# A two-layer graph attention kernel: the next step's exponentials taken directly behind ScalarE's copy of the sums

## The chip, the cores and the metric

One Trainium2 chip, one core of it. The metric is the device time of one execution in microseconds (us). The engines are named as the profile names them: PE is TensorE (PEld its weight loads), DVE is VectorE, ACT is ScalarE, POOL is GpSimd, SP is SyncE.

## What is computed

A graph with 6250 nodes and 106250 edges (50000 drawn edges in both directions and one loop per node), the edges sorted by their destination. A first stage applies a layer norm and a ReLU, a second one runs an equivariant convolution over all edges, and then two graph attention layers follow. The change touches only these last two, each of which computes, with 4 heads of 64 features:

```python
z = (x @ W).reshape(n, HEADS, ODIM)
el = jnp.sum(z * al, axis=-1)
er = jnp.sum(z * ar, axis=-1)
e = jax.nn.leaky_relu(el[src] + er[dst], negative_slope=NEG_SLOPE)
e_max = jax.ops.segment_max(e, dst, num_segments=n)
ex = jnp.exp(e - e_max[dst])
denom = jax.ops.segment_sum(ex, dst, num_segments=n)
alpha = ex / denom[dst]
msg = z[src] * alpha[:, :, None]
out = jax.ops.segment_sum(msg, dst, num_segments=n)
out = jax.nn.elu(out + x.reshape(n, HEADS, ODIM) + b.reshape(HEADS, ODIM))
```

## The kernel before, in words

The four stages (`front_stage`, `conv_stage`, `gat_stage` for layer 0 and for layer 1) run one after the other, each with a block of instructions of its own for every engine. In `gat_stage` the edges are taken in groups of 8 tiles of 128 edges, one group a step; a step adds its group's sums to a window of 128 nodes. A layer has 104 steps. Four steps make a quad, and a quad also finishes one block of 256 nodes, whose work is spread over its four steps r = 0 to 3. The loop (`all_steps`, L816 to L822) has one quad as its body, 25 times round, and the last quad is written out behind it, with `ahead` telling how many steps still follow. The order on each engine is written out by hand, and engines meet through semaphores alone.

Step v on each engine, as far as the change and the prediction speak of it:

- **POOL** (L1649 to L1657) gathers the rows of z for the step four ahead, in two groups of 4 indirect DMAs: the even tiles once PE has done its first half of the sums of the step whose buffer is reused (`half_summed`), the odd tiles once PE has done the second half (`part_summed`).
- **ACT** (L1605 to L1631) waits for `diff_ready` and takes two exponentials: L1609 of the 128 x 36 differences of score and maximum, which are the edges' weights `ex`, and L1610 of 36 x 1 values, the factor `fac` by which older sums are rescaled. Then it copies the transposed one-hots of step v + 2 (L1577), stages the indices of step v + 4 (L831), makes 8 weighted one-hots (L1619, for half of the odd tiles), waits until PE has summed the whole step, and copies PE's sums out of PSUM (L1624). Behind the copy stand the node block's work, which are three passes over 128 x 512 at r = 1 (L1581, L1583, L1585, the ELU's exponential) and in layer 0 one copy of table rows at r = 2 and at r = 3 (L1591), and the staging of step v + 4 (L839, L840, L842).
- **DVE** (L2011 to L2054) waits for the first exponential, makes the other weighted one-hots (L1927: two instructions for the first half of the sums, one for the second), folds the step before into its window (L1934 to L1943), and prepares the steps ahead: one-hots (L1855, L854), scores (L1880, L1883), the segment maxima by scans, the differences of step v + 1 (L1919, which raises `diff_ready`), and the first scans of step v + 2 (L1890, L1891). At r = 0 it takes the denominators' reciprocals early in the step and the node block's state at its end.
- **PE** (L1802 to L1828) makes the sums of the 8 tiles in two halves, `tile_sums` (16 matmuls at L1732 and 4 at L1737 each). The first half needs DVE's two weighted one-hots, and stands behind the window sums of the step before (L1746, L1748) and a small one for the scans (L1697); the second half needs DVE's third and ACT's eight. Between the halves stand L1705, L1684 and L1677. Behind the second half, L1711 hands DVE the transposed maxima of step v + 1.

So a step's differences are ready only shortly after PE has finished the sums of the step before, which is what ACT's copy waits for too.

Of the kernel before, what the change touches and what calls it, by code (L numbers as in the profile page):

```python
# [20 lines left out]
ACT = mybir.ActivationFunctionType  # L21
# [1349 lines left out]
def gat_stage(nc, m, layer):  # L1371
# [8 lines left out]
    with ExitStack() as ctx:  # L1380
# [3 lines left out]
        def sb(name, shape, dt=F32):  # L1384
            return ctx.enter_context(nc.sbuf_tensor(f"ge{layer}_" + name, shape, dt))
# [12 lines left out]
        def scratch(width, parts=P):  # L1398
            a = m.scratch[0:parts, free_scratch[0]:free_scratch[0] + width]
            free_scratch[0] += width  # L1400
            assert free_scratch[0] <= SCRATCH
            return a
# [22 lines left out]
        diff = [scratch(LANES) for u in range(2)]  # L1425
        ex = [scratch(LANES) for u in range(2)]
# [5 lines left out]
        fd = [sb(f"fd{u}", [LANES, 1]) for u in range(2)]  # L1432
        fac = [sb(f"fac{u}", [LANES, 1]) for u in range(2)]
# [137 lines left out]
        @block.scalar  # L1571
        def _(act):
            last_quad = load_last_quad(act, m)

            def copy_hotT(v):
                act.wait_ge(hotT_ps, v + 1)
                nc.scalar.copy(hotT, ps_hotT[:, 0:2 * P]).then_inc(hotT_ready, 1)  # L1577

            def exponential(k, b=node):
                act.wait_ge(s_v, k + 1)  # L1580
                nc.scalar.activation(b.h, b.x, ACT.Relu, scale=-1.0).then_inc(s_neg, 1)  # L1581
                act.wait_ge(s_neg, k + 1)
                nc.scalar.activation(b.h, b.h, ACT.Exp, scale=-1.0).then_inc(s_ex, 1)  # L1583
                act.wait_ge(s_ex, k + 1)
                nc.scalar.activation(b.ps[:, :], b.h, ACT.Copy, bias=-1.0).then_inc(s_em, 1)  # L1585

            def rows(k, t):
                act.wait_ge(s_pZ, k * 2 + (t + 1))
                if t == 0:
                    act.wait_ge(st_rows, k * 16 + 16)  # L1590
                nc.scalar.copy(node.rows[:, t * ZW:(t + 1) * ZW], ps_node[:, 0:ZW]).then_inc(s_rows, 1)  # L1591

            def last_rows(k, t, b):
                act.wait_ge(s_pZ, k * 2 + (t + 1))
                if t == 0 and b is node:
                    act.wait_ge(st_rows, k * 16 + 16)
                nc.scalar.copy(b.rows[:, t * ZW:(t + 1) * ZW], b.tables[t][:, 0:ZW]).then_inc(s_rows, 1)

            groups = [stage_sources(nc, act, m, r, idx[r], idx_ready) for r in range(4)]
            for r in range(4):  # L1600
                stage_places(nc, act, m, r, groups[r], staged[r], columns[r], staged_ready)
            for v in range(2):
                copy_hotT(v)

            def step(quad, r, ahead):  # L1605
                v = quad * 4 + r
                u = r % 2
                act.wait_ge(diff_ready, v + 1)
                nc.scalar.activation(ex[u], diff[u], ACT.Exp).then_inc(ex_ready, 1)  # L1609
                nc.scalar.activation(fac[u][:, :], fd[u][:, :], ACT.Exp).then_inc(ex_ready, 1)  # L1610
                if ahead >= 2:
                    copy_hotT(v + 2)
                if ahead >= 4:
                    group = stage_sources(nc, act, m, v + 4, idx[r], idx_ready)
                act.wait_ge(part_summed, v + 4)
                act.wait_ge(ex_ready, v * 2 + 2)
                for k in range(G // 2 + 1, G, 2):
                    for h in range(HEADS):
                        ins = nc.scalar.activation(weighted(k, h), one_hot(r, k), ACT.Copy,  # L1619
                                                   scale=ex[u][:, h * (G + 1) + k:h * (G + 1) + k + 1])  # L1620
                ins.then_inc(hots_act_ready, 1)
                act.wait_ge(part_summed, v + 5)
                act.wait_ge(summed, v + 1)
                nc.scalar.copy(sums, ps_part[:, 0:D + HEADS]).then_inc(sums_ready, 1)  # L1624
                if r == 1:
                    exponential(quad)
                if r >= 2 and layer == 0:
                    rows(quad, r - 2)
                if ahead >= 4:
                    act.wait_ge(pick_ready, v + 1)  # L1630
                    stage_places(nc, act, m, v + 4, group, staged[r], columns[r], staged_ready)  # L1631

            all_steps(act, last_quad, step)
            first, lead = load_rest(act, m, last_quad)
            with act.Fori(first, REAL, 2) as n:
                k = n + lead
                exponential(k)
                exponential(k + 1, second)
                if layer == 0:
                    for t in range(2):  # L1640
                        last_rows(k, t, node)
                    for t in range(2):
                        last_rows(k + 1, t, second)
# [488 lines left out]
```

## Time and profile before

| | us |
|---|---|
| three runs | 4824.91, 4825.26, 4829.48 |
| their median | 4825.26 |
| span of the profiled execution, first to last instruction | 4824.0 |
| first start of a layer 0 gather (L1655) | 1904.1 |
| ACT busy in the span | 1279.2 |
| POOL busy in the span | 2537.5 |

No time of its own is listed for the profiled execution beside its span; the span lies 1.26 us under the median of the runs. In the profile an operation is named by its line, engine and kind, then what it writes and reads (the small buffers all lie in `scratch`, the gathered rows in `nodes`). A row of the timeline gives its start, its duration, and in brackets how long the engine had been idle before it and what ended that; several like instructions in a row are merged (x8), and matmuls of 32-bit data count twice. "remote" in the brackets means that the profile found no engine's instruction that ended the wait at that time, "issue" that it found no wait at all. Ends of matmuls are modelled.

### The profile page before, as it was taken

What the parts mean: (1) busy time and instruction counts of PE and PEld (TensorE: products, weight loads), DVE (VectorE), ACT (ScalarE), POOL (GpSimd) and SP (SyncE); (2) the same over time, 40 slices, a digit from 0 to 9 for tenths busy, and PEclk for the clock granted to TensorE, in tenths of its full rate; (3) what the DMA queues carried; (4) which work ended last, traced back from release to release, by engine and by line L of the source; (5) the groups of instructions that cost most, each with busy time, mean ns of one, the idle gap of its engine ahead of it and who ended that gap; (6) DMA issues with size and microseconds to landing.
All of it is one profiled execution on the core that took longest, in us unless ns stands there. A gap on an engine that the chain in (4) does not pass through costs nothing. (4 is left out here: it accounts for less than half of the span.)

```text
span 4824.0 us, 104766 instructions
## 1 busy us (share of the span) xinstructions
PE 3342.4 (69%) x33932; PEld 2406.6 (50%) x33933; DVE 2350.8 (49%) x7219; ACT 1279.2 (27%) x4694; POOL 2537.5 (53%) x2630
## 2 busy tenths in 40 slices
PE   6567766676667775677777776666576776767676
PEld 4334444444444444455555555555455555555555
DVE  6445444444544444445444444444344554444455
ACT  5112211212212212233333333323222222222232
POOL 6444444444444443555555555553655555555553
PEclk9777777777777777555555555555555555555555
DMA  7222222222222222333333333332333333333332
GB/s 231 78 79 83 78 75 80 80 79 81 81 78 81 77 80 84 88 99 94 94 98 93 98 96 94 96 94 75 96 93 102 94 94 94 97 99 93 94 93 82
DMA packets 241750, 442.92 MB, mean 92 GB/s; under 512 B 83665, under 2 KB 134933, under 8 KB 241567
## 3 DMA queue, kind: packets, MB, share of 16 engines
q0 software_dynamic: 119808, 334.13, 25.4%
q1 hardware_dynamic: 121887, 108.14, 7.3%
q8 instruction: 25, 0.41, 0.0%
q14 instruction: 30, 0.25, 0.0%
HBM read 381.95 MB, written 60.10 MB: 92 GB/s over the span
## 5 line engine op out<-in xcount | busy, mean ns | idle before, releaser
L1655 POOL DMA_INDIRECT nodes<-z_rows,scratch x1664 | 1644.4, 988 | 1272.8 <-issue 415.7
L1101 POOL DMA_INDIRECT scratch<-h_rows,scratch x832 | 818.8, 984 | 941.7 <-DVE nodes L1251 716.0
L1732 PE MATMUL ge_part<-nodes,scratch 128*32 128x64 f32 x13312 | 472.6, 313 | 243.2 <-DVE scratch L1927 133.5
L1624 ACT COPY scratch<-ge_part 128x260 f32<-128x260 f32 x208 | 78.3, 376 | 1851.5 <-remote 1665.8
L1145 PE MATMUL ce_part<-nodes,scratch 128*32 128x128 f32 (+1 forms) x6656 | 456.7, 394 | 126.2 <-issue 113.4
L1732 PEld LDWEIGHTS ge_part<-nodes,scratch 128*32 128x32 f32 x13312 | 359.4, 167 | 296.5 <-issue 153.2
L1145 PEld LDWEIGHTS ce_part<-nodes,scratch 128*32 128x32 f32 x6656 | 256.5, 140 | 331.5 <-issue 279.2
L1279 DVE TENSOR_TENSOR nodes<-nodes,ce_sum 128x512 f32 x105 | 72.3, 689 | 707.6 <-remote 367.0
L1737 PE MATMUL ge_part<-scratch 128*32 128x4 f32 x3328 | 209.9, 200 | 261.5 <-issue 259.3
L1746 PE MATMUL ge_sum<-scratch 128*128 128x128 f32 x832 | 243.6, 445 | 208.4 <-ACT scratch L1624 208.2
L1919 DVE TENSOR_TENSOR scratch<-scratch,ge_runs 128x32 f32<-128x32 f32 x208 | 44.0, 212 | 692.4 <-remote 675.5
L1125 PE MATMUL ce_w<-fc_sb,scratch 64*128 64x256 f32 x1664 | 304.2, 495 | 109.3 <-ACT scratch L1020 96.3
L1155 PE MATMUL ce_sum<-nodes 128*128 128x128 f32 x832 | 167.5, 364 | 305.7 <-issue 217.6
L1251 DVE TENSOR_TENSOR nodes<-ce_w,scratch 128x768 f32<-128x768 f32 x416 | 377.2, 949 | 0.0
L1619 ACT ACTIVATE scratch<-scratch 128x32 f32<-128x32 f32 x1664 | 376.3, 312 | 0.1
L1927 DVE TENSOR_TENSOR scratch<-scratch 128x256 f32<-128x256 f32 x624 | 244.3, 419 | 233.8 <-ACT ge_fac L1610 137.3
L1125 PEld LDWEIGHTS ce_w<-fc_sb,scratch 64*128 64x128 f32 x1664 | 183.3, 236 | 277.0 <-issue 175.2
L1737 PEld LDWEIGHTS ge_part<-scratch 128*32 128x32 f32 x3328 | 187.8, 166 | 263.9 <-issue 261.5
L1155 PEld LDWEIGHTS ce_sum<-nodes 128*128 128x128 f32 x832 | 141.8, 257 | 349.1 <-issue 247.6
L1746 PEld LDWEIGHTS ge_sum<-scratch 128*128 128x128 f32 x832 | 184.4, 309 | 228.8 <-ACT scratch L1624 227.0
L1059 ACT COPY nodes<-ce_part 128x512 f32<-128x512 f32 x104 | 61.0, 586 | 804.5 <-remote 738.0
L1717 PEld LDWEIGHTS ge_sum<-ge_fac,lane_sel 36*128 36x128 f32 x832 | 184.0, 306 | 80.9 <-issue 76.5
(269 smaller groups left out, 5802.1 us busy)
## 6 DMA issues: line engine op xcount, KB each, us to landing
nodes<-z_rows,scratch POOLq DMA_INDIRECT x1664
nodes<-hT SPq DMA_DIRECT2D x56, 256.0 KB
scratch<-h_rows,scratch POOLq DMA_INDIRECT x832
z_rows<-scratch SPq DMA_DIRECT2D x28, 264.0 KB
z_rows<-nodes SPq DMA_DIRECT2D x28, 264.0 KB
hT<-scratch SPq DMA_DIRECT2D x28, 256.0 KB
hT<-nodes SPq DMA_DIRECT2D x28, 256.0 KB
nodes<-x_rows SPq DMA_DIRECT2D x28, 256.0 KB
```

Of the source, the lines that this page charges most:

```text
L1101: nc.gpsimd.indirect_dma_start(xg[u][:, i * D:(i + 1) * D], None, m.h_rows, bass.IndirectOffsetOnAxis(ap=idx[r][:, k:k + 1], axis=0)).then ...
L1125: ins = nc.tensor.matmul(ps_w[q][:, 2 * half + a, :, :].rearrange("p k f -> p (k f)"), hidT[u][rows, col:col + P], m.fc1[rows, :], start=T ...
L1145: ins = nc.tensor.matmul(here, hots[u][:, at:at + TW], these, start=(q == 0 and c == 0), stop=(q == 1), skip_group_check=True)
L1155: ins = nc.tensor.matmul(ps_sum[:, c, :], sums[:, c * P:(c + 1) * P], pick[u], start=(c == 0), stop=True, skip_group_check=True)
L1251: ins = V.tensor_tensor(out[:, :, 1 + 3 * k:4 + 3 * k, :], w[:, :, 2 + k:3 + k, :].broadcast_to([P, UNIT, 3, MUL]), x[:, :, 1:4, :], ALU.mult)
L1619: ins = nc.scalar.activation(weighted(k, h), one_hot(r, k), ACT.Copy, scale=ex[u][:, h * (G + 1) + k:h * (G + 1) + k + 1])
L1655: nc.gpsimd.indirect_dma_start(zg[r][:, k * ZW:(k + 1) * ZW], None, m.z_rows[layer], bass.IndirectOffsetOnAxis(ap=idx[r][:, k:k + 1], axis ...
L1717: nc.tensor.matmul(ps_sum[u][:, FAC + c:FAC + c + 1], m.lane_sel[:, c * P:(c + 1) * P], fac[u][:, :], start=(c == 0), stop=True, skip_grou ...
L1732: ins = nc.tensor.matmul(ps_part[j * TW:(j + 1) * TW, h * HF:(h + 1) * HF], weighted(k, h), zg[r][:, k * ZW + h * HF:k * ZW + (h + 1) * HF ...
L1737: ins = nc.tensor.matmul(ps_part[j * TW:(j + 1) * TW, D:D + HEADS], one_hot(r, k), lanes(ex[r % 2])[:, k, :], start=False, stop=(q == 1), ...
L1746: nc.tensor.matmul(ps_sum[u][:, c * NW:(c + 1) * NW], sums[:, c * P:(c + 1) * P], pick[u], start=False, stop=True, skip_group_check=True)
L1927: return V.tensor_tensor(out, one.broadcast_to([P, NB // 2, HEADS, TW]), by.broadcast_to([P, NB // 2, HEADS, TW]), ALU.mult)
```

## The change

The two exponentials become a helper. They are taken once for step 0 ahead of the loop, and then in step v for step v + 1, directly behind the copy of the sums and ahead of the node block's work and the staging, in place of standing first in the next step.

```diff
--- before.py
+++ after.py
@@ -1602,12 +1602,16 @@
             for v in range(2):
                 copy_hotT(v)
 
+            def exponentials(v, u):
+                act.wait_ge(diff_ready, v + 1)
+                nc.scalar.activation(ex[u], diff[u], ACT.Exp).then_inc(ex_ready, 1)
+                nc.scalar.activation(fac[u][:, :], fd[u][:, :], ACT.Exp).then_inc(ex_ready, 1)
+
+            exponentials(0, 0)
+
             def step(quad, r, ahead):
                 v = quad * 4 + r
                 u = r % 2
-                act.wait_ge(diff_ready, v + 1)
-                nc.scalar.activation(ex[u], diff[u], ACT.Exp).then_inc(ex_ready, 1)
-                nc.scalar.activation(fac[u][:, :], fd[u][:, :], ACT.Exp).then_inc(ex_ready, 1)
                 if ahead >= 2:
                     copy_hotT(v + 2)
                 if ahead >= 4:
@@ -1622,6 +1626,8 @@
                 act.wait_ge(part_summed, v + 5)
                 act.wait_ge(summed, v + 1)
                 nc.scalar.copy(sums, ps_part[:, 0:D + HEADS]).then_inc(sums_ready, 1)
+                if ahead >= 1:
+                    exponentials(v + 1, 1 - u)
                 if r == 1:
                     exponential(quad)
                 if r >= 2 and layer == 0:
```

Semaphores and buffers are the same, and the order on PE, DVE, POOL and SP is what it was. Names of lines shift: L1609 and L1610 become L1607 and L1608, L1619 becomes L1623, L1624 becomes L1628, and lines behind them grow by 6.

ACT, layer 0, from the last instruction ahead of the loop into its first step; before:

```order
L818 UNCONDITIONAL_BRANCH
L818 ISA
L1609 ACT_TABLE_LOAD
L1609 ACTIVATE scratch<-scratch 128x36
L1610 ACTIVATE ge_fac<-ge_fd 36x1
L1576 REGISTER_ALU
L1577 COPY scratch<-ge_hotT 128x256
L131 ISA
L131 TENSOR_LOAD tab
```

and now:

```order
L1577 COPY scratch<-ge_hotT 128x256 x2
L1607 ACT_TABLE_LOAD
L1607 ACTIVATE scratch<-scratch 128x36
L1608 ACTIVATE ge_fac<-ge_fd 36x1
L818 UNCONDITIONAL_BRANCH
L818 ISA
L1577 COPY scratch<-ge_hotT 128x256
L131 ISA
L131 TENSOR_LOAD tab
```

Exponentials and the load of ACT's function table in front of them (ACT_TABLE_LOAD) stood inside the loop, behind the branch at L818, and now stand ahead of it; no table load is left inside the loop. In layer 1 there was none and there is none.

ACT, layer 0, end of step r = 1 and start of the next: the staging and the exponentials before (the three node passes L1581 to L1585 stand between the copy L1624 and these rows),

```order
L839 ACTIVATE scratch<-dst_sb,minus_base 128x8
L840 ISA
L840 ACTIVATE scratch<-first,minus_base 128x5
L842 ISA
L842 COPY scratch<-pick_cols 128x128
L1609 ACTIVATE scratch<-scratch 128x36
L1610 ACTIVATE ge_fac<-ge_fd 36x1
L1577 COPY scratch<-ge_hotT 128x256
```

and now, from the copy of the sums on:

```order
L1628 COPY scratch<-ge_part 128x260
L1607 ACTIVATE scratch<-scratch 128x36
L1608 ACTIVATE ge_fac<-ge_fd 36x1
L1580 REGISTER_ALU
L1581 ACTIVATE nodes<-nodes 128x512
L1583 ACTIVATE nodes<-nodes 128x512
L1585 ACTIVATE ge_node<-nodes 128x512
```

The two exponentials have moved up past the node passes and the staging; the copy of the one-hots (L1577) follows the staging directly.

## Rows read from the trace of the kernel before

**Rows 1.** The page, part 1: busy time and share of each engine.
```profile
PE 3342.4 (69%) x33932; PEld 2406.6 (50%) x33933; DVE 2350.8 (49%) x7219; ACT 1279.2 (27%) x4694; POOL 2537.5 (53%) x2630
```

**Rows 2.** Waits of engines, one for another, 2505 to 3160 us (layer 0).
```profile
ACT scratch L1624 <- remote: 418.8, 45, 12.0
DVE scratch L1919 <- remote: 172.8, 45, 4.1
```

**Rows 3.** Timeline of ACT, layer 0: start us, us, operation.
```profile
2518.89 0.38 ACT L1624 COPY scratch<-ge_part 128x260 f32<-128x260 f32 x1 [9.70 <-remote]
...
2521.80 0.23 ACT L1609 ACTIVATE scratch<-scratch 128x36 f32<-128x36 f32 x1
...
2522.38 1.81 ACT L1619 ACTIVATE scratch<-scratch 128x32 f32<-128x32 f32 x8
2532.47 0.38 ACT L1624 COPY scratch<-ge_part 128x260 f32<-128x260 f32 x1 [8.28 <-remote]
...
2545.96 0.38 ACT L1624 COPY scratch<-ge_part 128x260 f32<-128x260 f32 x1 [9.62 <-remote]
```

**Rows 4.** Timeline of DVE over the same stretch.
```profile
2518.93 0.21 DVE L1919 TENSOR_TENSOR scratch<-scratch,ge_runs 128x32 f32<-128x32 f32 x1 [3.81 <-remote]
...
2519.44 0.39 DVE L1891 TENSOR_TENSOR_SCAN scratch<-scratch,ge_eT 36x128 f32<-36x128 f32 x1
2522.15 0.82 DVE L1927 TENSOR_TENSOR scratch<-scratch 128x256 f32<-128x256 f32 x2 [2.33 <-ACT ge_fac L1610]
```

**Rows 5.** Timeline of PE over the same stretch.
```profile
2521.00 0.39 PE L1697 MATMUL ge_runs<-perm,scratch 36*1 36x36 f32 x4
2523.03 1.08 PE L1732 MATMUL ge_part<-nodes,scratch 128*32 128x64 f32 x32 [1.64 <-DVE scratch L1927]
...
2527.11 1.08 PE L1732 MATMUL ge_part<-nodes,scratch 128*32 128x64 f32 x32
...
2535.12 1.08 PE L1732 MATMUL ge_part<-nodes,scratch 128*32 128x64 f32 x32 [0.17 <-issue]
```

**Rows 6.** Timeline of POOL over the same stretch.
```profile
2519.67 0.95 POOL L1655 DMA_INDIRECT nodes<-z_rows,scratch  x1 [1.87 <-remote]
...
2523.44 1.06 POOL L1655 DMA_INDIRECT nodes<-z_rows,scratch  x1 [0.30 <-issue]
2526.55 0.95 POOL L1655 DMA_INDIRECT nodes<-z_rows,scratch  x1 [2.05 <-PE ge_part L1737]
...
2530.33 0.95 POOL L1655 DMA_INDIRECT nodes<-z_rows,scratch  x1 [0.31 <-issue]
```

**Rows 7.** Timeline at the end of layer 0, past the last gather.
```profile
3314.24 1.04 POOL L1655 DMA_INDIRECT nodes<-z_rows,scratch  x1 [0.30 <-issue]
...
3328.31 1.08 PE L1732 MATMUL ge_part<-nodes,scratch 128*32 128x64 f32 x32
...
3329.52 0.38 ACT L1624 COPY scratch<-ge_part 128x260 f32<-128x260 f32 x1 [5.43 <-PE ge_part L1737]
```

**Rows 8.** L1609 over the whole run: duration ns min/median/max, first and last start.
```profile
L1609 ACT ACT_TABLE_LOAD  x25: 1283/1283/1283, 1917.8 to 3256.7; - x25
```

**Rows 9.** Timeline of ACT: copies 48 steps apart, in layers 0 and 1.
```profile
2505.37 0.38 ACT L1624 COPY scratch<-ge_part 128x260 f32<-128x260 f32 x1 [8.58 <-remote]
...
3159.59 0.38 ACT L1624 COPY scratch<-ge_part 128x260 f32<-128x260 f32 x1 [8.51 <-remote]
...
3968.96 0.38 ACT L1624 COPY scratch<-ge_part 128x260 f32<-128x260 f32 x1 [9.44 <-remote]
...
4621.76 0.38 ACT L1624 COPY scratch<-ge_part 128x260 f32<-128x260 f32 x1 [9.45 <-remote]
```

**Rows 10.** Timeline of DVE at a turn of the loop, layer 0 and layer 1.
```profile
2549.13 0.76 DVE L1927 TENSOR_TENSOR scratch<-scratch 128x256 f32<-128x256 f32 x2 [2.21 <-issue]
...
3794.58 0.76 DVE L1927 TENSOR_TENSOR scratch<-scratch 128x256 f32<-128x256 f32 x2 [1.26 <-ACT ge_fac L1610]
```

**Rows 11.** L1655 over the whole run, durations ns min/median/max.
```profile
L1655 POOL DMA_INDIRECT nodes<-z_rows,scratch x1664: 951/957/1622, 1904.1 to 4776.1; - x185
```

## The prediction

> **What bounds the kernel now.** I read the page first. No engine is full: over the span PE shows 69% and POOL 53%, and ACT, the engine that is reordered, 27% [rows 1]. ACT is thus short of work, and the question is only whether its two exponentials stand on the path that sets the length of a step. The view of waits says what ACT spends its time on: in 655 us of layer 0 it sat 418.8 us in front of its copy of the sums, in 45 waits of up to 12 us each, ended by something that the profile calls remote; DVE sat 172.8 us in front of the differences, again 45 times [rows 2]. Both wait for PE to finish a step's sums, at the same moment: the copy starts at 2518.89, the differences at 2518.93 [rows 3, 4].
>
> Next I laid the timelines of one step side by side. I call an interval the time from one copy of the sums to the next. The interval from 2518.89 to 2532.47 follows r = 1, so that ACT's node passes and staging stand between the copy and the exponential at 2521.80 [rows 3]. DVE's weighted one-hots follow at 2522.15, after 2.33 us of idling that ACT ended [rows 4], and PE's first half of the sums at 2523.03, after 1.64 us of idling that DVE ended [rows 5]. That is a visible chain from the exponential to PE, and it is what the change shortens.
>
> But what comes behind it does not follow PE's start. The second half starts at 2527.11 [rows 5] and the copy that waits for it only at 2532.47 [rows 3], 5.36 us later. Where no gather is running any more, behind the last of layer 0 at 3314.24, the same second half goes from 3328.31 to its copy at 3329.52, in 1.21 us [rows 7]. So some 4 us of every second half are not PE's own work. What stands beside them is POOL: its group of four gathers begins at 2526.55, the last of them begins at 2530.33 and ends at 2531.28 [rows 6], and 1.19 us after that end the copy is released. The group before runs from 2519.67 to 2524.50, and the group behind it starts 2.05 us later, released by PE [rows 6]. POOL thus alternates: four gathers at a pace of 1.26 us, PE's release about a microsecond behind their end, 2 us of gap, the next four. Two groups are (2530.33 - 2526.55) + (2523.44 - 2519.67) + 0.95 + 1.06 = 9.56 us, two gaps of about 2 us make the rest of 13.6. I read this as a step that is set by the gathers: PE's sums end when a group of gathers has drained, however long ago they were started. The trace doesn't say by what means the gathers hold PE back, and the forecast doesn't need it.
>
> **A test that lies in the trace.** The next interval, from 2532.47 to 2545.96, follows r = 2. ACT has less in front of its exponential there, and PE starts the first half at 2535.12 [rows 5], 2.65 us behind the copy, against 4.14 us in the interval before. PE is 1.49 us earlier and the interval is 13.49 us long against 13.58 [rows 3]: 0.09 us for 1.49.
>
> **The change, part by part.**
>
> 1. *Exponentials at r = 1, both layers (26 intervals each, 52).* The copy ends at 2519.27, the differences at 2519.14 [rows 3, 4], so the exponential will start around 2519.4 and not at 2521.80, some 2.4 us earlier. DVE is occupied with its scans until 2519.83 [rows 4], so its one-hots start near 2519.9. PE ends what stands in front of its sums at 2521.39 [rows 5]; that is late next, and the first half can start 2523.03 - 2521.39 = 1.64 us earlier. On the path this would be 52 x 1.64 = 85 us. By the test above it is nothing, or at the most 1.64 x 0.09/1.49 = 0.10 us an interval, 5 us in all. I take 0: the group of gathers ends at 2524.50, behind the time at which PE's first half, started at 2523.03 and 1.08 us long, stops showing work.
> 2. *Exponentials at r = 2 and r = 0.* At r = 2 PE starts the sums at 2535.12 with 0.17 us of idling [rows 5]; there is nothing to win but that. At r = 0 DVE has the node block's state in front of the one-hots, which the change leaves alone. 0.
> 3. *The turn of the loop (r = 3), layer 0.* The change takes 25 loads of ACT's function table, 1.283 us each, out of the loop [rows 8] and leaves one ahead of it. ACT is relieved by 24 x 1.283 = 31 us. At the turn DVE idles 2.21 us in front of the one-hots in layer 0 and 1.26 us in layer 1, where there is no table load [rows 10]; so DVE will be about 0.95 us earlier in layer 0. What the earlier start is worth is shown by the two layers: 48 steps of layer 0 take 3159.59 - 2505.37 = 654.22 us, the same number of layer 1 takes 4621.76 - 3968.96 = 652.80 us [rows 9]. The difference, 1.42 us in 12 quads, is 0.118 us a quad and 3.0 us in 25 quads. It holds everything in which the layers differ, the copies of table rows too, so 3.0 is at the upper end of what fits the pace of the gathers; a lower end is 0, and 31 us if each load were on the path. I take 3.0, since its row is of the very same step without the load.
> 4. *What is pushed back.* At r = 1 the node passes and the staging now start behind two short exponentials and a possible wait for the differences. The total of ACT's work up to the eight one-hots is the same, these therefore stay near 2522.4 to 2524.2, and the second half that needs them starts at 2527.11 [rows 3, 5]: 2.9 us of cover. Were that cover gone, each us of delay would count in full. The indices that POOL needs are staged ahead of these eight, four steps before their gathers. Where the differences come later than the copy, ACT waits for them with the staging and node work queued behind; ACT idles 8.28 us ahead of the next copy [rows 3], which hides this. 0. In the first step, and in the last four of each layer, gathers don't hide everything; there PE's own queue is next, and I take 0 with 1 us either way.
> 5. *Order on POOL, SP, PE.* No instruction of theirs moves, no DMA is issued earlier or later by order. 0.
>
> The sum: 4824.0 - 3.0 = 4821.0 us for the profiled span. The median of the runs stands 1.26 us over that span, so **4822 us**.
>
> Here the page and the Trainium skill differ on one price. The trace has the table load at 1.283 us [rows 8], and the exponential behind it is delayed by that and no more, as far as DVE's 0.95 us tell. The Trainium skill, "ScalarE: Activation LUTs", section "What ACT_TABLE_LOAD costs", gives the same 1283 ns and adds a drain of about 1380 ns, 2.66 us for each switch of set; by it ACT would be relieved by some 64 us and not 31, and the sum would still be the same, since the term goes by the two layers' pace. The measured row decides.
>
> **The rivals.**
>
> *The exponentials are on the path (faster).* For it speaks the chain of rows 4 and 5, in which the idling of DVE and PE ends with ACT's exponential. Against it speak the 5.36 us against 1.21 us and the interval at r = 2. Price: 85 us from part 1, and 0.95 x 25 = 24 us at the turn of layer 0: 4825 - 109 = 4716 us.
>
> *The table loads count in full (faster).* If at the turn of the loop ACT and not the gathers set the time, 24 x 1.283 = 31 us go: 4825 - 31 = 4794 us. Against it: then a turn in layer 0 would cost over a microsecond more than in layer 1, and not 0.118.
>
> *DVE falls on POOL's gathers (slower).* Gathers take 0.951 us at the least, 0.957 in the middle, and 1.622 us in the worst case [rows 11]; one in the rows above took 1.06 [rows 6]. With DVE's one-hots up to 2.2 us earlier at r = 1, and 0.95 at the turn, DVE works beside other gathers than now. If in each of these 52 + 25 = 77 intervals one gather more grew by half the way to that worst case, 0.33 us, and POOL's groups set the pace, the kernel would take 77 x 0.33 = 25 us more: 4825 + 25 = 4850 us. It decides from the point where the growth falls into the second group, which nothing compensates. Against it: the same instructions already run beside gathers in all intervals, and there is as much chance of an overlap going away. The Trainium skill, "GPSIMD Engine Reference", section "1. Specifications", says that GpSimd shares its SBUF interfaces with VectorE and contends with instructions that have two SBUF inputs, which L1927 has; it is this rival's mechanism, and the spread of rows 11 agrees with it without proving it.
>
> **How the numbers follow.** A measurement of this kernel can tell about 0.2% from no change, 9.65 us: faster is under 4815.6, slower over 4834.9. The gathers' pace, as forecast: 0.81. Exponentials on the path, 4716: 0.06. Table loads in full, 4794: 0.05. DVE on the gathers, 4850: 0.08. The forecast's own range is from 4822 - 5 (part 1's upper end) - 2 - 3 of doubt in the turn, 4812, to 4822 + 3 (part 3 worth nothing) + 2, and the runs' own 4 us of spread, 4831. To take in a part of the slower rival, with some gathers grown, the range goes to 4836; below, to 4809. That leaves out the two faster rivals and most of the slower one, under 0.2. Chances: faster 0.13 (both faster rivals and the lowest edge of the forecast), slower 0.08, same 0.79.
>
> **What would show it.** In the changed profile at r = 1 the exponential should stand about 0.5 us behind the copy, DVE's one-hots about 1.0 us and PE's first half about 2.5 us, against 4.14 now. No table load should remain in the quads of layer 0. If I am right, the intervals are still 13.5 to 13.6 us long, PE's second half starts about 8.3 us behind the copy, and ACT's wait in front of its copy is longer by what it saved. I am wrong if the second half starts earlier with the first and the intervals shrink by more than 0.1 us, or if gathers of the second group show well over 1 us where they showed 0.96.

## The result, and the profile after

The changed kernel takes 4861.84 us (median of 4 runs, 4858.3 to 4878.06), the kernel before 4825.09 us beside it (4 runs, 4821.57 to 4829.48). The ratio is 1.0071, 95% interval 1.0048 to 1.0095: **slower by about 34 us**, where 4822 us and no change were forecast. The profiled execution took 4859.04 us with a span of 4857.2 us, 33.2 us over the span before.

Two names first. POOL's four gathers right behind a copy of the sums fetch the odd tiles; I call them the *odd group* (the expectations below say "second group"). The four after them are the *even group*. Both can be seen in [rows 6]: the odd one from 2519.67, the even one from 2526.55.

The page after, part 1, answers to [rows 1]:

```profile
PE 3343.5 (69%) x33932; PEld 2410.4 (50%) x33933; DVE 2341.0 (48%) x7219; ACT 1269.3 (26%) x4670; POOL 2595.6 (53%) x2630
```

All instruction counts but ACT's (24 table loads fewer) are those of before, ACT and DVE are busy for 10 us less, and POOL for 58.1 us *more*. The gathers themselves (timings of L1661, which was L1655; [rows 11] before) and the table loads ([rows 8] before), each line by its own view:

```profile
L1661 POOL DMA_INDIRECT nodes<-z_rows,scratch x1664: 951/957/1750, 1906.9 to 4805.0; - x185
```

```profile
L1607 ACT ACT_TABLE_LOAD  x1: 1283/1283/1283, 1920.8 to 1920.8; - x1
```

The shortest and the middle gather are what they were; so some few got longer. The timeline of POOL behind the copy at 2526.21, a copy of r = 1, shows which (start, duration, operation, idle before and what ended it):

```profile
2526.99 1.64 POOL L1661 DMA_INDIRECT nodes<-z_rows,scratch  x1 [1.63 <-remote]
2528.94 0.96 POOL L1661 DMA_INDIRECT nodes<-z_rows,scratch  x1 [0.31 <-issue]
...
2531.46 0.96 POOL L1661 DMA_INDIRECT nodes<-z_rows,scratch  x1 [0.30 <-issue]
2534.25 0.95 POOL L1661 DMA_INDIRECT nodes<-z_rows,scratch  x1 [1.83 <-remote]
...
2540.87 1.75 POOL L1661 DMA_INDIRECT nodes<-z_rows,scratch  x1 [1.89 <-remote]
```

It is the first gather of the odd group: 1.64 us where [rows 6] has 0.95, and 1.75 us behind the next copy. The timeline of DVE tells what stands beside it:

```profile
2526.24 0.21 DVE L1925 TENSOR_TENSOR scratch<-scratch,ge_runs 128x32 f32<-128x32 f32 x1 [3.59 <-remote]
2527.07 0.73 DVE L1933 TENSOR_TENSOR scratch<-scratch 128x256 f32<-128x256 f32 x2
2528.74 0.22 DVE L1903 TENSOR_TENSOR_SCAN scratch<-scratch,ge_runs 1x36 f32<-1x36 f32 x1 [0.94 <-PE ge_runs L1703]
```

DVE's two weighted one-hots begin 0.86 us behind the copy and 0.08 us behind the gather. Before, they began at 3.26 us [rows 3, 4], when that gather was long done. PE's timeline, and ACT's copies of the sums from here on:

```profile
2528.64 1.08 PE L1738 MATMUL ge_part<-nodes,scratch 128*32 128x64 f32 x32
...
2533.94 1.08 PE L1738 MATMUL ge_part<-nodes,scratch 128*32 128x64 f32 x32
```

```profile
2512.28 0.38 ACT L1628 COPY scratch<-ge_part 128x260 f32<-128x260 f32 x1 [11.51 <-PE ge_part L1743]
2526.21 0.38 ACT L1628 COPY scratch<-ge_part 128x260 f32<-128x260 f32 x1 [9.71 <-remote]
2526.49 0.23 ACT L1607 ACTIVATE scratch<-scratch 128x36 f32<-128x36 f32 x1
...
2540.09 0.38 ACT L1628 COPY scratch<-ge_part 128x260 f32<-128x260 f32 x1 [8.48 <-remote]
...
2548.19 0.38 ACT L1628 COPY scratch<-ge_part 128x260 f32<-128x260 f32 x1 [4.06 <-PE ge_part L1743]
...
2567.26 0.38 ACT L1628 COPY scratch<-ge_part 128x260 f32<-128x260 f32 x1 [11.56 <-PE ge_part L1743]
```

The exponential stands 0.28 us behind the copy and PE's first half 2.43 us, so at r = 1 everything that was to become earlier did. The intervals are now 13.93, 13.88, 8.10 and 19.07 us: a quad of 54.98 us. Before, the medians of the four intervals of layer 0 are 13.56, 13.55, 13.49 and 13.75, together 54.35. The short and the long one (27.17 us) are no longer than their two before (27.24); it is the other two that grew, by 0.3 to 0.4 us each. Such a pair of a short and a long interval is not new: in layer 0 of the trace of before, every third quad has one, behind r = 1 and r = 2 (the copies at 2409.67, 2419.09 and 2437.15 are 9.42 and 18.06 us apart). New is how often: of the 84 intervals counted below, 22 of layer 0 are shorter than 12.9 us, and 7 were before. DVE's and PE's lead is gone by the even group: that starts at 2534.25, 8.04 us behind the copy, against 7.66 in [rows 3, 6].

Where the 33.2 us lie, by the copies of each layer: 10.2 and 9.1 us in the 84 steps between the 13th and the 97th copy (layers 0 and 1), 3.3 us in the first 12 steps of the two, 8.9 us in the last 7, 2.3 us ahead of the first copy, where nothing was changed, and -0.6 us in what is left. The stretch ahead of the first copy comes and goes between executions: in the four profiles taken on the first chip below, which differ only behind it, it takes 1967.0 to 1986.1 us. So the 84 steps are the finer measure below (12 steps, or three quads, are a full period of the rhythm, and 84 are seven): from the 13th copy's start to the 97th copy's, 1145.0 and 1142.1 us before, 1155.2 and 1151.1 us after.

### The profile page after: what moved, and what is told of

It reads as the page before. It is cut to its first block and busy times, and to the rows that moved or that the text cites. A ratio compares the mean times of both kernels' runs of the same rounds, so it can differ in the third digit from the quotient of the medians.

```text
span 4857.2 us, 104690 instructions
## 1 busy us (share of the span) xinstructions
PE 3343.5 (69%) x33932; PEld 2410.4 (50%) x33933; DVE 2341.0 (48%) x7219; ACT 1269.3 (26%) x4670; POOL 2595.6 (53%) x2630
## 5 line engine op out<-in xcount | busy, mean ns | idle before, releaser
L1661 POOL DMA_INDIRECT nodes<-z_rows,scratch x1664 | 1702.4, 1023 | 1240.8 <-issue 409.3
L1738 PE MATMUL ge_part<-nodes,scratch 128*32 128x64 f32 x13312 | 526.4, 313 | 220.5 <-issue 181.5
L1628 ACT COPY scratch<-ge_part 128x260 f32<-128x260 f32 x208 | 78.2, 376 | 1818.3 <-remote 1253.6
L1145 PE MATMUL ce_part<-nodes,scratch 128*32 128x128 f32 (+1 forms) x6656 | 443.7, 385 | 138.4 <-issue 123.9
L1738 PEld LDWEIGHTS ge_part<-nodes,scratch 128*32 128x32 f32 x13312 | 385.1, 165 | 299.0 <-issue 258.3
L1623 ACT ACTIVATE scratch<-scratch 128x32 f32<-128x32 f32 x1664 | 375.3, 308 | 8.6 <-issue 8.5
L1690 PE MATMUL ge_er<-scratch 128*128 128x16 f32 x832 | 219.7, 359 | 83.0 <-issue 81.7
L1690 PEld LDWEIGHTS ge_er<-scratch 128*128 128x128 f32 x832 | 202.7, 315 | 93.0 <-issue 89.0
L1743 PE MATMUL ge_part<-scratch 128*32 128x4 f32 x3328 | 165.5, 203 | 104.4 <-issue 103.4
```

The lines of the kernel that those rows point to most:

```text
L1145: ins = nc.tensor.matmul(here, hots[u][:, at:at + TW], these, start=(q == 0 and c == 0), stop=(q == 1), skip_group_check=True)
L1661: nc.gpsimd.indirect_dma_start(zg[r][:, k * ZW:(k + 1) * ZW], None, m.z_rows[layer], bass.IndirectOffsetOnAxis(ap=idx[r][:, k:k + 1], axis ...
L1690: ins = nc.tensor.matmul(ps_er[:, q * W:(q + 1) * W], hotT[:, q * P:(q + 1) * P], er4, start=(q == 0), stop=True, skip_group_check=True)
L1738: ins = nc.tensor.matmul(ps_part[j * TW:(j + 1) * TW, h * HF:(h + 1) * HF], weighted(k, h), zg[r][:, k * ZW + h * HF:k * ZW + (h + 1) * HF ...
L1743: ins = nc.tensor.matmul(ps_part[j * TW:(j + 1) * TW, D:D + HEADS], one_hot(r, k), lanes(ex[r % 2])[:, k, :], start=False, stop=(q == 1), ...
```

## The experiments

**Theory 1**: DVE's two weighted one-hots (each a product of two operands in SBUF), moved over the first odd gather, stretch it, and the gathers set the pace. **Theory 2**: PE's earlier first half is what costs. **Theory 3**: the loss is made at the turn of the loop, or by the table load's new place. The runs come from three chips: the first four of the table from one on which the kernel before takes 4839.9 us, the next four from a second (4737.2 us), and the last eight, in two sets, from a third (4734.8 and 4732.0 us). Each ratio is against runs of the kernel before in the same set. Profiles are compared within a set, or between the last two chips, whose speed is the same; the first chip has no profile of the kernel before, and only_r3 stands in for it.

| run | first odd gather, us | 84 steps, layers 0 and 1, us | ratio, 95% interval |
|---|---|---|---|
| only_r3 | 0.95 | 1142.9, 1140.8 | 1.0011 (0.9998 to 1.0025) |
| only_r1 | 1.64 | 1150.5, 1147.9 | 1.0029 (1.0012 to 1.0047) |
| only_r2 | 1.74 | 1148.7, 1144.1 | 1.0044 (1.0031 to 1.0058) |
| hold | 1.64 | 1155.5, 1149.5 | 1.0074 (1.0052 to 1.0097) |
| x_two | 1.30 | 1128.7, 1126.1 | 0.9991 (0.9981 to 1.0001) |
| x_psum | 0.95 | 1127.9, 1125.6 | 0.9994 (0.9981 to 1.0008) |
| psum_before | 0.95 | 1128.0, 1127.0 | 0.9997 (0.9985 to 1.0008) |
| psum_after | 0.95 | 1128.4, 1127.6 | 1.0006 (0.9993 to 1.0019) |
| before_again | 0.95 | 1127.5, 1124.7 | - |
| after_again | 1.64 | 1138.1, 1133.5 | 1.0069 (1.0049 to 1.0088) |
| psum_after_again | 0.95 | 1128.4, 1128.2 | 1.0004 (0.9992 to 1.0017) |
| x_same | 1.30 | 1128.3, 1127.3 | 1.0006 (0.9996 to 1.0016) |
| x_next | 1.30 | 1128.1, 1127.0 | 1.0001 (0.9989 to 1.0012) |
| x_long | 2.31 | 1145.2, 1142.1 | 1.0084 (1.0065 to 1.0102) |
| only_r1_again | 1.64 | 1133.6, 1134.2 | 1.0050 (1.0034 to 1.0067) |
| psum_r3 | 0.95 | 1127.9, 1127.1 | 1.0014 (1.0003 to 1.0024) |

(The gather is the median behind the copy that the experiment is about: r = 2 in only_r2, the turn in only_r3, r = 1 in the others. In only_r2 it is 1.74 us in two quads of three and 0.95 us in the third. Kernels without the loss differ by up to 3.5 us in the 84 steps of a layer from one profile to the next in the same set, so less than that says nothing.)

**Which part of the change costs.** The helper's early call is kept for one r alone, the others stand where they stood before (here r = 1; only_r2 and only_r3 likewise):

```diff
             def step(quad, r, ahead):
...
+                if r in (1, 3, 0, ):
+                    exponentials(v, u)
...
-                if ahead >= 1:
+                if ahead >= 1 and r in (1, ):
                     exponentials(v + 1, 1 - u)
```

> Exponentials early only at the turn of the loop (behind r = 3), which also takes ACT's table load out of the loop. Theory 1 (DVE's one-hots run over the first gather of POOL's second group and stretch it): at the turn DVE is held by its own branch until about 2.2 us behind the copy, so nothing collides; first gather of the group 0.95 to 1.0 us, time 4819 to 4825 us. Theory 2 (the first half of the sums ends before the gathers block PE, and the regrouped pauses cost): PE starts at about 3.1 us here, too late for that; same time. Theory 3 (the early exponentials at the turn or the moved table load are the loss): 4840 to 4862 us.

> Exponentials early only behind r = 1; all others, and the table load in the loop, as before. Theory 1: the first gather behind this copy grows from 0.95 to about 1.6 us, 52 times, 35 us of POOL time, of which the pauses give some back: 4840 to 4855 us. Theory 2: the first half of the sums ends 3.5 us behind the copy instead of 6.6, the interval behind r = 2 turns short and the one behind r = 3 long, and that costs most of the loss: 4845 to 4862 us. Theory 3: 4825 us.

> Exponentials early only behind r = 2. Theory 1: DVE's one-hots start 0.95 us behind the copy instead of 1.65 and meet the first gather of the group: it grows to about 1.5 us, while now the second of the group is the one that grows (to 1.1 or 1.2): net 0.3 us times 52, 4835 to 4842 us. Theory 2: PE starts at 2.42 instead of 2.5 to 2.65 us; if it ends before the gathers block it, the loss is as large as with r = 1. Theory 3: 4825 us.

The turn (only_r3), where the table load goes and where the first odd gather stays at 0.95 us, costs nothing that the runs can tell: theory 3 falls. r = 1 and r = 2 each cost, and each has its stretched first odd gather. The costs of only_r1 and only_r2 add up to 0.73%, about the whole.

The two costs arise in different places. In only_r1 the interval behind r = 1 itself grows, to a median of 13.84 us in layer 0 where only_r3 has 13.50. In only_r2 the intervals behind the stretched gather do not: where it takes 1.74 us, those behind r = 2 and r = 3 of layer 0 are about 8.4 and 18.6 us, together 27.0 us, and only_r3 has 27.2 us there. What grows is the interval behind r = 0 of the next quad. DVE comes to it late: its pair begins 4.7 us behind the copy and not 3.1, and the work that it does behind the pair then stands beside the first *even* gather. Timelines of only_r2 behind the copy of r = 0 at 2369.16, of POOL and of DVE:

```profile
2377.04 1.49 POOL L1661 DMA_INDIRECT nodes<-z_rows,scratch  x1 [2.38 <-PE ge_part L1743]
2378.83 0.95 POOL L1661 DMA_INDIRECT nodes<-z_rows,scratch  x1 [0.30 <-issue]
```

```profile
2373.89 0.75 DVE L1933 TENSOR_TENSOR scratch<-scratch 128x256 f32<-128x256 f32 x2
...
2377.09 0.27 DVE L1861 TENSOR_TENSOR scratch<-drop,scratch 128x128 f32<-128x128 f32 x1
2377.29 0.41 DVE L854 TENSOR_TENSOR scratch<-cols,scratch 128x256 f32<-128x256 f32 x1
```

The 14 intervals of layer 0 with such an even gather take 14.02 us on average, the other 7 take 13.55 us; in layer 1 it is 14 at 14.02 and 7 at 13.52. The changed kernel has the same in 15 and 12 of its 21 quads. So at r = 2 the loss is not paid where the pair now lies, but two intervals later, in the even group. Why a stretch at r = 2 turns the rhythm to short and long is not shown, and that L1861 and L854, both with two operands in SBUF, are what stretches the even gather is read from their place only.

**A repair that repaired nothing.** In the changed kernel DVE was to wait until POOL had issued that gather:

```diff
+                        if k == 1:
+                            pool.sem_inc(first_out, 1)
...
                 dve.wait_ge(part_summed, v + 4)
+                if ahead >= 3 and r in (0, 1, 2, 3):
+                    dve.wait_ge(first_out, v + 4)
                 weighted_one_hots(r, 0)
```

> The changed kernel, and DVE's weighted one-hots wait in addition until POOL has issued the first gather of its second group (one more semaphore). Theory 1: the first gather of the group is back at 0.95 us, DVE's one-hots start about 1.9 us behind the copy, the whole loss is gone: 4818 to 4828 us. Theory 2: PE starts its first half near 2.7 us, behind the point at which it can end early, so it also gives about 4825 us; this run tells them from theory 3 and from a cost of the early exponentials on ACT, which would leave 4850 to 4862 us.

The one-hots still began 0.86 us behind the copy, beside a gather of 1.64 us: POOL's increment did not wait for the gather in front of it to end. The experiment says nothing on the theories, and is a repeat of the changed kernel (1.0074).

**The stretch made in the kernel before.** At the end of step r = 1, DVE makes two more 128x256 products there, into memory that nobody reads; once with both operands in SBUF and once with the second in PSUM:

```diff
+                if r in (1,):
+                    for half in range(2):
...
+                        by = score[0].rearrange("p (h e o) -> p e h o", h=HEADS, o=1)[:, 0:G:2][:, tiles]
+                        V.tensor_tensor(dum[:, half * 256:half * 256 + 256].rearrange("p (a h n) -> p a h n", a=2, h=HEADS), one.broadcast_to([P, NB // 2, HEADS, TW]),
+                                        by.broadcast_to([P, NB // 2, HEADS, TW]), ALU.mult)
```

> The kernel before, with two more DVE products of 128 x 256 at the end of its step r = 1, of the shape of the weighted one-hots, both operands in SBUF, result unused. DVE was idle there for over 2 us, ACT's exponentials and PE's sums stay where they were. Theory 1 (collision of DVE and the gather): the first gather behind the copy of r = 1 grows from 0.95 to about 1.6 us as in only_r1, and the 84 middle steps of a layer take as much longer as there, 5 to 6 us (1145.0 and 1142.1 before). Theory 2 (PE's earlier first half is what costs): PE is not earlier, so no change: 1145 and 1142 us.

> The same two extra products, but the second operand comes from PSUM, so that DVE reads SBUF with one operand only. If two SBUF operands are what blocks the gather, it stays at 0.95 us and the 84 middle steps at 1145 and 1142 us; if any DVE product that reads and writes SBUF blocks it, it grows to 1.6 us as in x_two.

Timeline of POOL behind a copy of r = 1, in x_two and then in x_psum:

```profile
2502.58 1.30 POOL L1656 DMA_INDIRECT nodes<-z_rows,scratch  x1 [1.72 <-remote]
```

```profile
2504.03 0.95 POOL L1656 DMA_INDIRECT nodes<-z_rows,scratch  x1 [1.76 <-remote]
```

and of DVE, in the same order:

```profile
2502.66 0.73 DVE L2057 TENSOR_TENSOR nodes<-scratch 128x256 f32<-128x256 f32 x2
```

```profile
2504.11 0.72 DVE L2058 TENSOR_TENSOR nodes<-scratch,ge_eT 128x256 f32<-128x256 f32 x2
```

Same shape, same length, both 0.08 us behind the gather's start; only the one with two SBUF operands lengthens it. That much of theory 1 is shown. But the gather grew by half of what the change makes of it, and the kernel did not get slower, where theory 1 had 5 to 6 us a layer: a miss.

**The change without the overlap's cause.** A second exponential leaves the weights in PSUM too, and DVE's first two one-hots read them there (psum_after on the changed kernel, psum_before on the one before):

```diff
+        ps_ex = ps_part[:, 320:320 + LANES]
...
+                nc.scalar.activation(ps_ex, diff[u], ACT.Exp).then_inc(ex_ready, 1)
...
-                by = ex[r % 2].rearrange("p (h e o) -> p e h o", h=HEADS, o=1)[:, q:G:2][:, tiles]
+                by = (ex[r % 2] if q else ps_ex).rearrange("p (h e o) -> p e h o", h=HEADS, o=1)[:, q:G:2][:, tiles]
```

> The changed kernel, with a second exponential of the same differences written to PSUM (0.23 us more of ACT), from which DVE's first two weighted one-hots read their weights; the one-hots start as early as in the changed kernel, or 0.15 us later. Theory 1 with the condition of two SBUF operands: the first gathers behind r = 1 and r = 2 are back at 0.95 us and the loss of the 84 middle steps (1155.2 and 1151.1 us) goes, to 1140 to 1146 us and 1138 to 1143 us, and the kernel is level with the one before or a few us faster. Theory 2: PE's first half is as early as in the changed kernel, so 1150 to 1156 us stay.

> The kernel before, with the same second exponential in PSUM read by the first two one-hots. Theory 1: the small growth of gathers that is there already (31.3 us of gathers a quad in layer 0 against 32 x 0.951 = 30.4) goes in part: 1140 to 1144 us and 1138 to 1141 us for the 84 middle steps. Theory 2: no change but for 0.14 us of later one-hots, which the gathers cover: 1145 and 1142 us.

The loss was gone, but the changed kernel had not been run on that chip. So psum_after was repeated beside it, with the kernel before, and with x_same, a closer copy of the change's overlap: DVE makes its own pair of r = 1 a second time (`dve.wait_ge(part_summed, v + 5)`, `weighted_one_hots(r, 0)`, `weighted_one_hots(r, 1)`, at the end of step r = 1; a semaphore makes the real pair of r = 2 wait for it).

> The kernel before, to have its trace on the same chip as the three kernels run with it. Every theory: first gather of the second group behind the copy of r = 1 and r = 2 at 0.95 us; the 84 steps between the 13th and the 97th copy of a layer as before (1145.0 and 1142.1 us, or some 1 to 1.5% less on a faster chip).

> The changed kernel beside its own repair (psum_after_again) on one chip. Every theory: its loss is seen again, ratio 1.005 to 1.009 of before; first gathers of the second group at 1.64 us (r = 1) and 1.48 us (r = 2); 84 steps 9 to 10 us longer than those of before_again in each layer. If the ratio is under 1.002, the loss depends on the chip and what psum_after showed elsewhere is no evidence.

> The changed kernel, but the first two weighted one-hots read their weights from a copy in PSUM. Theory 1 (DVE's products with two SBUF operands stretch the gather, and this is the loss): first gathers at 0.95 us, 84 steps within 2 us of before_again's, ratio 0.998 to 1.002. Theory 2 (PE's earlier first half costs by itself): PE's first half is as early as in after_again (2.4 us), and so 84 steps are 9 us longer, ratio about 1.007.

> The kernel before, its ACT and PE as they were; DVE only makes its two weighted one-hots a second time behind step r = 1, where the changed kernel has the first pair (the values are of old weights and are overwritten by the real ones). Theory 1: the first gather of the second group behind r = 1 grows to about 1.64 us as in only_r1, and the 84 steps grow by 4 to 6 us a layer, ratio about 1.003. Theory 2: the gather may grow, but PE is as late as in before, and the 84 steps stay within 1 us; ratio 1.000.

Timelines of psum_after_again behind a copy of r = 1 at 2559.53, of POOL, DVE and PE:

```profile
2560.31 0.95 POOL L1663 DMA_INDIRECT nodes<-z_rows,scratch  x1 [1.74 <-remote]
```

```profile
2560.39 0.72 DVE L1935 TENSOR_TENSOR scratch<-scratch,ge_part 128x256 f32<-128x256 f32 x2
```

```profile
2561.95 1.08 PE L1740 MATMUL ge_part<-nodes,scratch 128*32 128x64 f32 x32
```

DVE's pair is as early as in the changed kernel (0.86 us), PE's first half too (2.42 us), the gather is 0.95 us again, and the time is that of the kernel before: 1.0004 against after_again's 1.0069 on the same chip. (Its 84 steps are 0.9 us over before_again's in layer 0 but 3.5 us in layer 1, where at most 2 us were expected; that is as far as kernels without the loss differ.) Short intervals are back at 7 in 84, and the even gather at r = 0 is back at 0.95 us, though only the pair was changed: the cost at r = 0 too begins with the pair. **Theory 2 falls**: PE's earliness by itself costs nothing. x_same missed: 1.30 us again and no loss, where theory 1 had 1.64 us and 1.003.

**How much stretch it takes.** Is the stretched gather enough for a loss, or does it take PE's earlier half as well? In the kernel before, x_next makes at the end of r = 1 the very pair that the change puts there, that of r = 2 with old weights; x_long adds the two products of x_two behind it. In both, a semaphore (`twice`) also holds the real pair of r = 2, and ACT's exponential before it, until the extra pair is done.

```diff
+                if r == 1:
+                    dve.wait_ge(part_summed, v + 5)
+                    weighted_one_hots(2, 0)
+                    weighted_one_hots(2, 1).then_inc(twice, 1)
```

> The kernel before, in which DVE makes the very two weighted one-hots of step r = 2 (same one-hots, same buffers, old weights) 0.86 us behind the copy of r = 1, and again at their place with the right weights. x_same, with the pair of r = 1, stretched the gather by 0.35 us and not by 0.69, and cost nothing. Theory 1 (the stretched gather is enough): the first gather shows 1.64 us, the interval behind r = 1 grows by 0.2 to 0.3 us and the 84 steps by 4 to 6 us a layer, as in only_r1_again. Theory 1b (the stretch costs only together with PE's earlier half): gather 1.64 us, but 84 steps within 1.5 us of the kernel before. If the gather stays at 1.30 us the pair's operands are not what makes the difference.

> As x_next, with two more DVE products of two SBUF operands behind the pair, 1.5 us in all. Theory 1: the gather or its follower grows by up to 1.4 us and the interval behind r = 1 grows with it, by over 0.5 us; 84 steps 10 us or more over before's. Theory 1b: the group of gathers is longer by as much, but the intervals stay within 0.1 us.

> Exponentials early at r = 1 only, the comparison for x_next on the same chip. Every theory: as before, first gather 1.64 us, PE's first half at 2.4 us, 84 steps 5 to 6 us longer in each layer, ratio 1.002 to 1.004.

Timelines of POOL, first x_next (copy at 2568.62), then x_long (copy at 2473.05):

```profile
2569.40 1.30 POOL L1658 DMA_INDIRECT nodes<-z_rows,scratch  x1 [1.76 <-remote]
...
2573.68 0.95 POOL L1658 DMA_INDIRECT nodes<-z_rows,scratch  x1 [0.30 <-issue]
2576.27 0.95 POOL L1658 DMA_INDIRECT nodes<-z_rows,scratch  x1 [1.63 <-remote]
```

```profile
2473.83 2.31 POOL L1659 DMA_INDIRECT nodes<-z_rows,scratch  x1 [1.75 <-remote]
...
2479.03 1.22 POOL L1659 DMA_INDIRECT nodes<-z_rows,scratch  x1 [0.30 <-issue]
2481.61 0.95 POOL L1659 DMA_INDIRECT nodes<-z_rows,scratch  x1 [1.36 <-remote]
```

and of PE in x_long:

```profile
2477.03 1.08 PE L1736 MATMUL ge_part<-nodes,scratch 128*32 128x64 f32 x32 [1.48 <-DVE scratch L1931]
```

x_long's exponentials are where they were before, PE's first half starts 3.98 us behind the copy (4.14 before), and it loses 0.84%, more than the change. So **a stretched gather is enough without an earlier PE**, if the stretch is as long as this. Put in order of where the odd group ends, all behind r = 1 in layer 0, medians in us from the copy (all on chips of one speed):

| run | odd group ends | even group starts | 84 steps of layer 0 |
|---|---|---|---|
| before_again | 5.62 | 7.59 | 1127.5 |
| psum_after_again | 5.91 | 7.63 | 1128.4 |
| x_next | 6.01 | 7.64 | 1128.1 |
| x_two | 6.10 | 7.63 | 1128.7 |
| only_r1_again | 6.20 | 7.93 | 1133.6 |
| x_long | 7.20 | 8.56 | 1145.2 |

Up to 6.10 us the even group doesn't move; at 6.20 it is 0.3 us late and at 7.20 1 us. The odd group has 0.5 us of slack, and then a late end is paid. This fits that x_two, x_same and x_next cost nothing and only_r1 does. But one thing more lies between 6.10 and 6.20: PE's first half begins 4.0 to 4.1 us behind the copy in x_two, x_next and x_long, and at 2.42 us in only_r1. No run has a gather of 1.64 us with PE's half as late as before, so theory 1b, that a stretch of this size costs only together with PE's earlier half, is not excluded for the change itself. What sets 7.6 us where the group ends early is not settled either. (In psum_after_again the end is at 5.91 us since the last odd gather takes 1.35 us there, and 1.07 before.) Nor is why the same pair at the same place stretches a gather by 0.35 us in x_next and by 0.69 us in only_r1: its operands and its 0.08 us of distance are the same.

**The best of both**, exponentials early at the turn alone and the first pair's weights in PSUM:

> The version that should be best if the theories hold: exponentials early at the turn of the loop alone (no table load in it), weights of the first one-hots in PSUM. Gathers at 0.95 us behind the copy; 84 steps 1 to 2 us shorter than those of the kernel before; ratio 0.998 to 1.001, so the runs may not tell it from no change.

The first odd gathers are all at 0.95 us, but the 84 steps are those of the others and not 1 to 2 us shorter, and the ratio is 1.0014, if anything slower: a miss. No version here beats the kernel before.

## Why the prediction was wrong

- **Part 1, the exponentials at r = 1, is the step that failed.** It argued that the early start wins nothing, which held: 2.42 us against a forecast of 2.5 for PE, and no gain in any run. It then took 0 for the part's cost as well, as if an early start that wins nothing could lose nothing. The interval at r = 2 of before, its test, had the one-hots 1.84 us behind the copy; the change puts them at 0.86 to 0.97, on to a gather that begins at 0.78. No row of the test covered that. The trace of before could have warned: the gather that DVE's pair meets is the one that is longer. At r = 2 the pair begins at 1.84 us and the second odd gather has 1.06 us (median, layer 0; 1.21 in layer 1), at the turn it begins at 3.17 us and the third has 1.12 us, and their neighbours have 0.95 to 0.96. Measured, only_r1 costs 0.29% and, repeated, 0.50%: 14 and 24 us where 0 stood.
- **Part 2, r = 2: 0 was taken, and it cost 0.44%, some 21 us.** "PE can win only 0.17 us" was true and beside the point: what mattered was DVE's start, from 1.84 to 0.97 us behind the copy and so on to POOL's gather, not PE's. The time itself is lost behind r = 0, which the same part had at 0 too, since the change "leaves alone" what DVE does there: it does, but DVE gets there 1.6 us later, and its work falls on the even group.
- **Part 3, the turn.** 3.0 us were to be won in layer 0. only_r3 shows 2.1 us less than the first profile of before (perhaps another chip's) in layer 0's 84 steps and 1.3 us less in layer 1's, where there was no table load, both inside what profiles differ by; the runs show 1.0011. The term was at best what it was called and can't be told from nothing. In the trace of before, the exponential behind a load begins 1.29 us after the load does (2602.40 and 2603.69), so the drain that the Trainium skill ("ScalarE: Activation LUTs", "What ACT_TABLE_LOAD costs") adds to its 1283 ns doesn't show there.
- **Part 4, what is pushed back**, held: the second half of PE at r = 1 starts 7.73 us behind the copy (8.22 before) and isn't delayed by ACT's eight one-hots. The 8.9 us in the last seven steps of the two layers, where 1 us of doubt was given, were not taken apart; on one chip after_again has 4.7 us there over before_again and psum_after_again 0.3 us, so they go with the same cause.
- **Part 5, POOL**: no instruction moved, and its cost was still not 0. An engine's own order is not all that sets its time.
- **The base held.** The gathers set the pace: the step follows the gathers when they grow (x_long) and follows PE not at all when PE is 1.7 us earlier (psum_after). Neither of the two faster rivals shows in any run.
- **The slower rival was the right one**, put at 0.08, far too low. Its 4850 us came near (4862), but by other terms, and so in part by luck: not 77 gathers by 0.33 us, but each of r = 1 by 0.69 us, two of three at r = 2 by 0.79, about as many even ones at r = 0 by 0.54, no first one at the turn, and a part of it swallowed by slack. It was put down on the argument that as many overlaps go as come. But those that went had cost little: the last odd gather had 1.06 us, 0.11 over its floor [rows 6], and the one that came costs 0.69. The rival decides, it said, once the growth falls into "the second group". Read as the odd group, the second in which a step's gathers are issued, this is what r = 1 does, from half a microsecond on; read as the even group, it is what r = 0 does. The sign named for being wrong, gathers well over 1 us, is the one that came. The rule of the Trainium skill, "GPSIMD Engine Reference", section "1. Specifications", of contention with DVE instructions of two SBUF inputs, spoke against this change; x_two against x_psum now agrees with it, 1.30 against 0.95 us.

## What to carry to other kernels

When an engine off the path is made earlier, lay its new place over the timeline of the engine that sets the pace, instruction by instruction: a stretch costs nothing while there is slack, and from there on it is paid (an odd group that ends 0.6 us later moved the next one by 0.3 us, one that ends 1.6 us later by 1.0). Then follow the engine into the next steps too: at r = 2 the early pair cost nothing where it lay, and 0.5 us two intervals later. Two operands in SBUF on DVE beside a gather on POOL are such a case, and one operand in PSUM takes it away. "Wins nothing" is not "costs nothing"; each needs its own row.

## What the runs showed that was not expected

- Two DVE products of 0.73 us in all, begun 0.08 us behind a gather of 0.95 us, lengthen it to 1.30 or 1.64 us; four, over 1.4 us, to 2.31 us (x_long); with one operand in PSUM not at all (x_psum, psum_after).
- POOL's semaphore increment that stands behind a gather did not hold DVE back until that gather's end (hold).
- PE does not carry the benefit of an early start through a group of gathers: its first half is started 1.7 us earlier in psum_after_again, and the even group that waits for it starts at 7.63 us against 7.59.
- The steps have a rhythm of three quads, with one short and one long interval even before the change, and a lengthened group can make more of them: the changed kernel had 8.10 and 19.07 us in a row, x_long 10.67 and 16.78 us. The first pair is no longer than two even steps (27.2 us before), the second 0.8 us longer (26.65 us on its chip), so the length of a single interval misleads, and only sums over whole quads, best over three, can be compared.
- The cost can lie away from its cause: in only_r2 it is the even gather behind r = 0, 1.49 us long, and not the odd one behind r = 2, 1.74 us long.
